# Four bias products of 32 rows each, one silu over 2048 columns, and newly laid orders in a cross-attention and feed-forward kernel

## What is computed

```python
x = x + xattn(layernorm(x), ctx, mask)      # softmax(x.ctx^T / sqrt(512), masked) @ ctx
x = x + ffn(layernorm(x), w1, b1, ln_g, ln_b, w2, b2)

def bitlinear158(x, w, b):                  # ternary weights, activations rounded to 8 bits
    return act_quant(rms_norm(x)) @ weight_quant(w).T + b

def ffn(x, w1, b1, ln_g, ln_b, w2, b2):
    h = silu(bitlinear158(x, w1, b1))       # 128 x 2048
    h = gelu(h)                             # the exact one
    h = layer_norm(h, ln_g, ln_b)
    return bitlinear158(h, w2, b2)          # 128 x 512
```

## Time and profile before

| | before |
|---|---|
| timed runs, us | 422.11, 418.84, 419.87 |
| median, us | 419.87 |
| profiled execution, us | 421.23 |
| its span, first to last instruction, us | 419.40 |
| mean granted TensorE clock in it | 0.983 |
| busy PE / DVE / ACT / POOL, us | 384.0 / 365.9 / 381.8 / 271.8 |

### The profile page before, as it was taken

One profiled execution on the slowest core, in us unless ns is written; L12 is line 12 of the kernel. 1 busy time (PEld: TensorE's weight loads), 2 busy tenths in 40 slices (PEclk: granted clock), 3 DMA queues, 4 the chain that ended last, 5 costly groups with the idle time before them and its releaser, 6 DMA issues.

```text
span 419.4 us, 6830 instructions
## 1 busy us (share of the span) xinstructions
PE 384.0 (92%) x1878; PEld 204.7 (49%) x1878; DVE 365.9 (87%) x571; ACT 381.8 (91%) x517; POOL 271.8 (65%) x373
## 2 busy tenths in 40 slices
PE   3899988789999999999999999999999987899996
PEld 2667353535545544544555454554455532344342
DVE  5278669989998989999999999989998789999992
ACT  1497999999999999999999999999999999999960
POOL 5358488764687838764785569585468855477930
PEclk9999998899999999999999999999999996999999
DMA  7998992556755677669668757694654423083484
GB/s 278 409 312 301 359 342 69 153 162 142 211 147 131 188 193 184 103 189 204 155 169 249 190 166 148 199 222 107 174 135 106 91 63 63 2 200 102 87 214 128
DMA packets 110389, 73.87 MB, mean 176 GB/s; under 512 B 87048, under 2 KB 87056, under 8 KB 109584
## 3 DMA queue, kind: packets, MB, share of 16 engines
q1 hardware_dynamic: 110352, 73.43, 65.1%
HBM read 44.05 MB, written 8.39 MB: 125 GB/s over the span
## 4 chain that ended last, share of the span: by engine, by line
issue 25%; ACT 21%; DVE 19%; PE 17%; POOL 13%; DMA 4%; SPq 1%; DVEq 0%; POOLq 0%; ACTq 0%
ACT junk_v L1212 6%; DVE hid L1981 5%; DVE hid L1972 5%; PE z L624 4%; PE acc L649 4%; ACT hid L1201 3%; ACT hid L1207 3%; POOL hid L1618 3%; PE ba L574 3%; ACT junk_l L1223 2%; POOL rstd L1607 2%; DVE am L1986 2%; POOL xc L1563 2%; DVE st L1900 1%; DMA hid<-in_w2T_dram 1%
## 5 line engine op out<-in xcount | busy, mean ns | idle before, releaser
L624 PE MATMUL z<-w1q,q1T 128*128 128x512 f16 x512 | 124.0, 386 | 3.3 <-ACT hid L1201 3.1
L649 PE MATMUL acc<-w2q,q2T 128*128 128x512 f16 x512 | 117.4, 379 | 0.4 <-DMA q2T<-hid 0.4
L1981 DVE SCALAR_TENSOR_TENSOR hid<-hid,rstd,beta 128x2048 f32<-128x2048 f32 x32 | 76.8, 2402 | 6.2 <-POOL rstd L1607 5.9
L624 PEld LDWEIGHTS z<-w1q,q1T 128*128 128x128 f16 x512 | 49.9, 99 | 65.6 <-ACT hid L1201 9.7
L1972 DVE SCALAR_TENSOR_TENSOR hid<-hid,nmu,gain 128x2048 f32<-128x2048 f32 x32 | 79.3, 2480 | 0.4 <-POOL nmu L1599 0.3
L649 PEld LDWEIGHTS acc<-w2q,q2T 128*128 128x128 f16 x512 | 49.8, 98 | 58.2 <-issue 0.9
L1986 DVE TENSOR_REDUCE am<-hid 128x1 f32<-128x2049 f32 x32 | 72.5, 2269 | 0.1
L1201 ACT ACTIVATE hid<-z,fac 128x1024 f32<-128x1024 f32 x64 | 70.7, 1119 | 1.6 <-PE z L629 1.4
L1223 ACT ACTIVATE junk_l<-hid 128x2050 bf16<-128x2050 f32 x32 | 61.1, 1910 | 4.1 <-DVE hid L1981 4.0
L1618 POOL TENSOR_SCALAR hid<-hid,kq 128x2048 f16<-128x2048 f32 x30 | 60.9, 2031 | 4.6 <-DVE kq L1993 3.1
L1212 ACT ACTIVATE junk_v<-hid,gsum 128x2048 bf16<-128x2048 f32 x32 | 63.7, 1990 | 0.1
(11 more groups left out here) (105 smaller groups left out, 572.2 us busy)
## 6 DMA issues: line engine op xcount, KB each, us to landing
ctxT<-in_ctxT_dram SPq DMA_DIRECT2D x32, 256.0 KB, 3.5
xs<-in_x_dram SPq DMA_DIRECT2D x32, 256.0 KB, 3.9
xT<-in_xT_dram SPq DMA_DIRECT2D x32, 256.0 KB, 3.6
ctx<-in_ctx_dram SPq DMA_DIRECT2D x32, 256.0 KB, 3.4
out_dram<-xs SPq DMA_DIRECT2D x32, 256.0 KB, 3.0
hid<-in_w1T_dram SPq DMA_DIRECT2D x4, 1024.0 KB, 10.2
hid<-in_w2T_dram SPq DMA_DIRECT2D x4, 1024.0 KB, 7.8
gain<-in_g_dram SPq DMA_DIRECT2D x1, 1024.0 KB, 11.1
```

What stands on the lines that cost most here:

```text
L624: pe.matmul(z_ps[h][:, c * CH:(c + 1) * CH], q1T[:, t % 4, k, :], w1q[:, k, f0:f0 + CH], start=(k == 0), stop=False)
L649: mm = pe.matmul(a, q2T[:, t % 2, c, :], w2q[:, c, :], start=False, stop=(c == FC - 1))
L1981: dve.scalar_tensor_tensor(out=hh, in0=hh, scalar=rstd[:, t:t + 1], in1=beta[:, :], op0=ALU.mult, op1=ALU.add).then_inc(s_l, 1)
```

## The change

b1's product is cut by rows of the array. The factor columns that split_factors writes are repeated in four bands of 32 columns, so that the turned factors stand on partitions 0, 32, 64 and 96; rows1 holds b1's four pieces of 512 columns in the same four bands; and the four products of a tile each take one band, 32 rows, into one bank each. They come after all sixteen products of the tile. z becomes one PSUM tensor of four banks with one semaphore, and silu one instruction of 2048 columns. first_product(t, 0) waits for the whole silu(t-1). copy_b1 copies 128 partitions of 512 columns. gelu_mean moves from POOL to DVE. The mask is loaded once; a column of the identity, repeated, picks its row. A silu of tiles 4 to 7 waits only for the w2 block whose place it takes. turn_factors no longer waits itself for the output two tiles back; that wait stands in the order. All five orders are new.

```diff
-        z_ps = [stack.enter_context(nc.psum_tensor(f"z{h}", [P, HALF], F32)) for h in range(2)]
+        z_ps = stack.enter_context(nc.psum_tensor("z", [P, FF], F32))
...
-                wait(pe, s_silu[h], t)
-                pe.wait_ge(s_q1T[t % 4], landed(t, 4))
+                if h == 0:
+                    wait(pe, s_silu, t)
+                    pe.wait_ge(s_q1T[t % 4], landed(t, 4))
                 for k in range(DC):
...
-                pe.wait_ge(s_brow, t + 1)
-                for c in range(2):
-                    f0 = h * HALF + c * CH
-                    mm = pe.matmul(z_ps[h][:, c * CH:(c + 1) * CH], brows[:, t % 4, :], rows1[:, f0:f0 + CH],
-                                   start=False, stop=True)
-                mm.then_inc(s_z[h], 1)
+                if h == 1:
+
+                    pe.wait_ge(s_brow, t + 1)
+                    for c in range(BANDS):
+                        band = slice(c * BAND, (c + 1) * BAND)
+                        mm = pe.matmul(z_ps[:, c * CH:(c + 1) * CH], brows[band, t % 4, :], rows1[band, :],
+                                       start=False, stop=True)
+                    mm.then_inc(s_z, 1)
...
-                act.activation(hid[:, t % HR, half(h)], z_ps[h][:, :], ACT.Silu, scale=fac[:, t, 0:1]).then_inc(s_silu[h], 1)
+                act.wait_ge(s_z, t + 1)
+                act.activation(hid[:, t % HR, 0:FF], z_ps[:, :], ACT.Silu, scale=fac[:, t, 0:1]).then_inc(s_silu, 1)
...
-                act.activation(rows1[0:ROWS, :], b1_ps, ACT.Copy).then_inc(s_rows[0], 1)
+                act.activation(rows1[:, :], b1_ps, ACT.Copy).then_inc(s_rows[0], 1)
...
-                pe.matmul(score_ps, ones_b[:, :], maskb[:, t // G % 2, t % G, :], start=True, stop=False)
+                pe.matmul(score_ps, ident_b[:, t:t + 1].to_broadcast((P, P)), maskb[:, :], start=True, stop=False)
...
-                wait(pe, s_o, b - 1)
-                wait(pe, s_brow, s)
+                wait(pe, s_brow, s if b <= 0 else s - 1)
...
-            def gelu_mean(t):
-                pool.wait_ge(s_gelu, t + 1)
-                pool.tensor_scalar(nmu[:, t:t + 1], gsum[:, t:t + 1], -1.0 / FF, 0.0,
-                                   ALU.mult, ALU.add).then_inc(s_nmu, 1)
...
+            def gelu_mean(t):
+                dve.wait_ge(s_gelu, t + 1)
+                dve.tensor_scalar(nmu[:, t:t + 1], gsum[:, t:t + 1], -1.0 / FF, None, ALU.mult).then_inc(s_nmu, 1)
```

More of the change, by code:

```diff
@@ L33 @@
 ROWS = PARTS * PARTS
+BAND = 32
+BANDS = P // BAND
 STEPS = 2
@@ L1003, in _ @@
-            scores(27)
-            second_product(16, 0)
+            pe.wait_ge(s_o, 16)
             turn_factors(23)
+            first_product(22, 1)
             pe.wait_ge(s_x1, 26)
@@ L1379, in _ @@
[L1379 to L1390 removed]
+            silu(8)
+            square_x1(10)
+            square_x1(11)
+            variance(7)
+            copy_probT(13)
+            square_l(4)
+            square_l(5)
+            silu(9)
@@ new lines, in _ @@
+            gelu(8)
+            gelu(9)
+            copy_probT(14)
+            mean_term(16)
+            silu(10)
+            square_x1(12)
+            square_x1(13)
+            mean_term(17)
+            square_l(6)
+            square_l(7)
+            variance(8)
+            copy_probT(15)
+            variance(9)
+            silu(11)
+            exp_scores(16)
+            exp_scores(17)
+            gelu(10)
+            gelu(11)
+            silu(12)
+            variance(10)
+            square_x1(14)
@@ new lines, in _ @@
+            square_x1(15)
+            variance(11)
+            copy_probT(16)
+            mean_term(18)
+            square_l(8)
+            square_l(9)
+            mean_term(19)
+            silu(13)
+            copy_probT(17)
+            gelu(12)
+            gelu(13)
+            exp_scores(18)
+            exp_scores(19)
+            variance(12)
+            silu(14)
+            variance(13)
+            mean_term(20)
+            mean_term(21)
+            square_l(10)
+            copy_probT(18)
@@ new lines, in _ @@
+            silu(15)
+            square_l(11)
+            square_x1(16)
+            square_x1(17)
+            copy_probT(19)
+            gelu(14)
+            gelu(15)
+            exp_scores(20)
+            exp_scores(21)
+            variance(14)
+            copy_probT(20)
+            silu(16)
+            variance(15)
+            square_x1(18)
+            square_l(12)
+            square_l(13)
+            square_x1(19)
+            mean_term(22)
+            mean_term(23)
+            silu(17)
@@ L1391, in _ @@
+            copy_probT(21)
+            gelu(16)
+            gelu(17)
+            exp_scores(22)
+            exp_scores(23)
+            variance(16)
+            silu(18)
+            variance(17)
+            square_l(14)
+            square_l(15)
+            silu(19)
+            mean_term(24)
+            copy_probT(22)
+            mean_term(25)
+            square_x1(20)
+            square_x1(21)
+            copy_probT(23)
             gelu(18)
             gelu(19)
+            exp_scores(24)
```

2020 lines of the change are left out of this document (915 added, 1105 removed).

## The result

The changed kernel takes 423.72 us (median of 4 executions, 423.32 to 427.3) beside 419.78 for the kernel before: a ratio of 1.011, 95% interval 1.0073 to 1.0147. So it is 0.6 to 1.1% slower, around the edge of what can be told from no change, and certainly not the 1.8% faster that was forecast. The profiled execution took 423.32 us with a span of 421.5, 2.1 more than before.

The account below looks back on a forecast made before the run. ScalarE (ACT) was taken as the bound, 98.7% busy from 80 to 320 us. Terms -8.7 (ACT), -0.5 (start) and +1.7 (waits) gave -7.5 us, so 412.4 us from a median of 419.87; range 405 to 420.

Parts of the forecast that it names:

- What ACT loses: ScalarE's work: silu saves 4.8 us, fewer table loads 2.6, the smaller b1 copy 1.3; together 8.7 us.
- What PE loses: TensorE's b1 products fall from 0.86 to 0.3-0.4 us per tile, saving about 0.5; off the path, so not counted.
- What z in one piece costs: Between two silus: z takes some 4.0 us from silu end to silu start, covered by at least 7 us of other work.
- it fits by 0.7 us: Tiles 10 to 11, the closest place found: PE needs 10.7 us between two z, ACT's work to the silu 11.4.
- The small waits of the steady part: ACT's idle share, 80 to 320 us, rises from 1.35% to 1.9%: +1.7 us over 320 us.
- DVE and POOL: gelu_mean on DVE adds 0.15 us per tile, 4.8 in all; DVE reaches 11.04 us per tile against ACT's 11.23.
- Rival B: DVE, together with POOL, becomes the bound; tiles take 11.44 us and the time is 416 to 420; chance 0.22.
- D: b1's four products on PE run one after the other and the array empties twice per tile: 419 to 421; chance 0.06.
- A: The main case: ACT stays the bound and its saved work becomes time, 405 to 416 us; chance 0.60.
- Rival C: Tiles in lockstep, ACT waiting for z and PE for silu in turn; slower, 427 us; chance 0.12.
- Start: Before the first silu: later mask and w1 loads against shorter steps and less ACT work; -0.5 us, between -3 and +2.
- Tail: From silu(31) to the end: the work is the same, so 0.

Follow-up runs that it names:

- e3: Changed kernel with each tile's silu split again into two instructions of 1024 columns, each with its own semaphore: 425.63 us, ratio 1.0138 to the kernel before.
- e10: Changed kernel with b1 again as four full 128-row products one after the other, its copy 2048 columns and the factors split for one band: 429.37 us, ratio 1.0218.
- e8: Kernel before with only b1's bands added, two products per half of z, with split, copy and rows to match: 422.26 us, ratio 1.0068.
- e7: Changed kernel with 22 idle TensorE products of 256 columns around tile 4, where TensorE stood: 421.80 us, ratio 1.0037 to the kernel before.
- e9: Changed kernel with idle TensorE products at four places where TensorE stood and its clock fell: 419.18 us, ratio 0.9994 to the kernel before.
- e15: Kernel of e9 with 15 more idle TensorE products at a fifth place, 51 to 54 us: 418.61 us, ratio 0.9976 to the kernel before.
- e12: Changed kernel as it is, timed again in 8 executions against the kernel before: 422.36 us, ratio 1.0064.
- e11: Kernel before with only gelu_mean moved from POOL to DVE, right ahead of gained: 420.76 us, ratio 1.0022.
- e4: Kernel before with z in one piece and one silu of 2048 columns at the second half's place, all old orders kept: 478.0 us, ratio 1.1383.

## Why the prediction was wrong

**What ACT loses: right.** Silu 1.963 us against 1.98; 17 + 17 + 11 + 1 = 46 table loads; the copy of b1 0.587 against 0.57. Together 7.3 us, 8.7 forecast: what is left for the silu is 7.3 - 2.6 - 1.3 = 3.4 where the term was 4.8. e3, which changes the silu alone, measures 4.6, so about 1.2 us lie elsewhere in ACT's work, and where isn't known. (The eight products of the earlier trace rows span 1.72 us, not 1.73; nothing hangs on it.)

**What PE loses: the size right, its value wrong.** The b1 products cost 0.42 us per tile, at the upper end of the 0.3 to 0.4 taken. "None of it counts in the sum, since PE was not on the path" failed: e10 puts the bands at 7 us in the new order, the copy of b1 and the clock included. In the old order, with two halves of z, they cost 2.7 (e8).

**What z in one piece costs: the step that failed.** The sum from silu end to silu start (4.0 us) and "it fits by 0.7 us" were worked out at full clock, at one place. It left out what the text itself had in the earlier trace rows: PE stands now and then and runs at half speed for some microseconds behind that. "PE can lose some 4 us once and nobody on the path sees it, since z is already waiting" held only while ACT had half a tile of z in hand; the change took that away. The 4.0 us become up to 8 at half clock, an estimate; at the place shown, with a readout between, it was 7.6 us. e7, e9 and e15 took about 4 us back in steps (3.2 of them, e9 against e12, clear of noise), and e15 is 1.0 us under the kernel before. The 7.3 us of work less are thus worth 1 us when the clock is kept up.

This is not the whole miss: e15 is still 6 us above the forecast of 412.4. In its profile ACT stands 3.6 us more than before the change: 2.1 before 40 us, 0.2 from 40 to 320 and 1.4 behind that. The small waits of the steady part, +1.7 in the sum, thus came out at 0.9 once the clock held. The start and the end weren't recovered by any run, and that profile (417.36 us) is itself shorter than the median of e15, so where the other 1.3 us lie isn't known.

**DVE and POOL: half right.** The mean on DVE costs 0.9 to 1.3 us (e11). DVE didn't become the bound: 93.7% from 80 to 320 us, not 97%. Rival B falls; so does D (0.42 us per tile, not 0.8); and A took the work that ACT lost for time. Rival C named the mechanism, with 0.12: it came at four or five places instead of at every pair, so +3 us instead of +7; and e4 is C in full. That the wider split costs nothing, since "POOL has a third of its time free", is doubtful after e8.

**Start: -0.5 was wrong in the profile.** The first silu came 3.0 us later (2.0 in e12), and by 40 us ACT had done 3.1 us less. ACT's last partial sum of w1 started at 26.23 instead of 24.78, as feared, and DVE stood for x(7), which the text didn't see. Moving that load's statistics did not lower the time.

**Tail: 0 was wrong by 1.7.** From silu(31) to the end 29.7 us instead of 28.0. Of PE's time there 1.2 is the half clock at 393.64, behind 6.3 us in which PE stood three times ahead of turning factors, 5.6 of it for POOL's split; the text looked at ACT and DVE only.

The range failed in part for the same reason: its cases treated the clock as a sign to look for, not as a price. With the clock kept up (e15, 418.6) the time lies inside 405 to 420, but still 6 us from the forecast.

## What to carry to other kernels

Before merging two buffers into one, add up the path from its release to its next use at the lower clock of TensorE too, and list the places where TensorE stands ahead of it: a buffer in hand is what hides a slow stretch. Where TensorE must stand ahead of work that is waited for, idle products in a free bank are cheap (12 in 1.47 us in e7, 0.12 each) and can be laid as long as the stand. An operation's saving depends on the order it lands in: the bands, with the split and the copy that go with them, cost 2.7 us in the old order and gave 7 in the new.

## What the runs showed of the hardware

Whether the clock falls behind a given stand differs between executions of one program (3.60 against 1.90 us for the same eight products, after the same 3.2 us of standing); what decides it stays open. Two concurrent products of 32 rows and 512 columns cost as much as four (0.32 us and 0.1 on entering): a pair gained nothing over one after the other, four gained 0.44 us, and three weren't tried. And POOL's small instructions can take ten times their time: in the tail the split's second step took 2.37 us where the median of its 21 is 0.23 (changed kernel, POOL's timeline), while DVE ran gained(30) from 389.27 to 391.61:

```profile
387.28 0.23 POOL L1497 TENSOR_TENSOR rest<-inv,bcols 128x16 f32<-128x16 f32 x1
...
389.34 2.37 POOL L1497 TENSOR_TENSOR rest<-inv,bcols 128x16 f32<-128x16 f32 x1
```

Both end within 0.1 us of each other; that DVE's instruction is the cause was not tested by a run of its own.
